# Attention on one Trainium2 core: heads paired in two 64-row halves of the array, a shared ring of three two-bank PSUM units, and q and k loaded per batch

## What is computed

```python
q = q.reshape(B, T, nh, hd)            # layer 0: rotated by cos, sin; layer 1: x @ Wq.T + bq
scores = jnp.einsum('bqhd,bkhd->bhqk', q, k) * scale + bias[None]   # the bias in layer 0 alone
attn = jax.nn.softmax(scores, axis=-1)
out = jnp.einsum('bhqk,bkhd->bqhd', attn, v)
```

## Time and profile before

| | us |
|---|---|
| median of 3 runs (lowest, highest) | 1241.4 (1240.12, 1244.76) |
| span of the profiled execution | 1240.9 |
| attention 0: until the first maxima, until the first scores, end | 53.6, 79.6, about 306 |
| attention 1: start, first maxima, first scores, last steps | 566, 621.5, 659.2, 912 |

### The profile page before, as it was taken

One profiled execution on the slowest core, in us unless ns is written; L12 is line 12 of the kernel. 1 busy time (PEld: TensorE's weight loads), 2 busy tenths in 40 slices (PEclk: granted clock), 3 DMA queues, 4 the chain that ended last, 5 costly groups with the idle time before them and its releaser, 6 DMA issues. The chain is left out here.

```text
span 1240.9 us, 15672 instructions
## 1 busy us (share of the span) xinstructions
PE 968.8 (78%) x5344; PEld 675.0 (54%) x5344; DVE 710.9 (57%) x1399; ACT 463.2 (37%) x702; POOL 350.5 (28%) x308
## 2 busy tenths in 40 slices
PE   0299999997609999973389999999976049999990
PEld 0144444453608999971245545656436038888880
DVE  6578888783610111108457777787614957667762
ACT  1026666666202323321015566565732104233320
POOL 7333333001051111113010101100010056888861
PEclk9999999999558999996568999999995559999995
DMA  9876655620338999954491555443005024454525
GB/s 191 150 141 124 115 80 108 83 31 10 109 140 293 342 336 353 337 210 148 95 145 30 102 82 106 70 58 54 7 1 204 0 81 119 111 148 128 122 37 152
DMA packets 83893, 159.87 MB, mean 129 GB/s; under 512 B 10088, under 2 KB 51944, under 8 KB 75624
## 3 DMA queue, kind: packets, MB, share of 16 engines
q1 hardware_dynamic: 74176, 142.13, 44.6%
q0 software_dynamic: 8384, 14.96, 5.7%
q10 hardware_dynamic: 1280, 2.10, 1.3%
HBM read 121.25 MB, written 35.80 MB: 127 GB/s over the span
## 5 line engine op out<-in xcount | busy, mean ns | idle before, releaser
L700 DVE TENSOR_REDUCE a_row_max<-ps_max 128x1 f32<-128x512 f32 x512 | 334.8, 686 | 95.5 <-PE ps_max L480 92.5
L594 ACT ACTIVATE a_probs<-ps_st 128x1024 f32<-128x1024 f32 x256 | 250.7, 1022 | 130.9 <-PE ps_st L496 129.2
L480 PE MATMUL ps_max<-a_ka,a_qa 96*128 96x512 f32 x512 | 221.2, 475 | 39.3 <-DMA a_ka<-scratch_k_scr 26.2
L480 PEld LDWEIGHTS ps_max<-a_ka,a_qa 96*128 96x128 f32 x512 | 96.8, 202 | 171.0 <-DVE a_row_max L700 124.2
L496 PE MATMUL ps_st<-a_qa,a_ka 104*128 104x512 f32 x512 | 173.7, 425 | 1.0 <-ACT a_probs L594 1.0
L510 PE MATMUL ps_out<-a_probs,a_vaug 128*32 128x512 f32 x1024 | 136.9, 607 | 0.4 <-ACT a_probs L594 0.4
L496 PEld LDWEIGHTS ps_st<-a_qa,a_ka 104*128 104x128 f32 x512 | 91.1, 193 | 23.4 <-ACT a_probs L594 8.7
L905 ACT ACTIVATE e_hid<-ps_st,e_wts 128x128 f32<-128x128 f32 x192 | 54.8, 369 | 114.6 <-PE ps_st L958 77.3
L1282 PE MATMUL ps_st<-e_xt,e_wr 128*128 128x512 f32 x384 | 93.6, 401 | 4.1 <-DVE e_xt L1344 2.7
L958 PEld LDWEIGHTS ps_st<-e_xst,e_wts 128*128 128x128 f32 x768 | 92.0, 196 | 2.2 <-issue 1.0
L958 PE MATMUL ps_st<-e_xst,e_wts 128*128 128x128 f32 x768 | 92.2, 280 | 0.6 <-DVE e_xst L1041 0.6
(11 more groups left out here) (184 smaller groups left out, 1149.4 us busy)
## 6 DMA issues: line engine op xcount, KB each, us to landing
e_wts<-in_w SPq DMA_DIRECT2D x24, 1156.0 KB, 8.1
e_wts<-in_w SPq DMA_DIRECT2D x24, 1024.0 KB
e_wf<-in_w SPq DMA_DIRECT2D x16, 1024.0 KB, 4.9
a_qa<-scratch_q_scr SPq DMA_DIRECT2D x96, 128.0 KB, 5.1
a_ka<-scratch_k_scr SPq DMA_DIRECT2D x96, 128.0 KB, 5.6
scratch_k_scr<-a_kst SPq DMA_DIRECT2D x16, 512.0 KB, 6.9
scratch_q_scr<-a_qst SPq DMA_DIRECT2D x64, 128.0 KB, 1.9
a_ctx_t<-in_ctx_t SPq DMA_DIRECT2D x8, 512.0 KB, 6.1
```

The lines of the kernel that those rows point to most:

```text
L480: pe.matmul(m.ps_max[:, n % 2], qa[0:MAX_ROW, g, h, qt * P:(qt + 1) * P], ka[0:MAX_ROW, g, h], start=True, stop=True).then_inc(mx_full, 1)
L594: nc.scalar.activation(probs[:, t % 3, 2 * pair:2 * pair + 2], m.ps_st[:, 2 * (n % 2):2 * (n % 2) + 2], ACT.Exp).then_inc(exp_done, 1)
L700: dve.tensor_reduce(row_max[:, s % 3, h, qt:qt + 1], m.ps_max[:, n % 2], AX.X, ALU.max).then_inc(mx_read, 1)
```

## The change

- A matmul now contracts 48 rows (52 with the bias), or 52 and 56 with the maxima rows. Even heads lie in partitions 0 to 63, odd heads in 64 to 127; the two matmuls of a pair follow each other, each in its own 64-row half, into the two banks of one unit.
- Six PSUM banks form a ring of three two-bank units, which maxima and scores take in turn. A unit is written once its user of three places before has been read. A DVE reduction reads both banks at once.
- Within a step the order is: maxima pair, scores pair, maxima pair, the first scores pair of the next step, `weigh`, then all jobs.
- q is handled in pairs of tiles (512 columns in `ps_misc`): ACT writes the high part, DVE the rest; POOL's subtraction is gone. In layer 0 the second pair of batch 0 is rotated by DVE. The scale moves from q into the exponential.
- `ka` and `qa` have two copies over batches and aren't cleared. Batch 0 is loaded by groups (12 DMAs of 64 KB each), every later batch at once (12 DMAs of 256 KB), and its first maxima wait for all twelve. SP, no longer ACT, issues the maxima rows, as two DMAs.
- The constant rows go in by six DMAs (two in layer 1) of 4 partitions and 128 KB from POOL at the start.
- The loads of x for batches 2 and 3 and the context of batch 1 are issued after the first loads of q and k; the statistics of batches 1 to 3 are computed in steps -5 and 4 (layer 0). The reciprocal root, in all four stages, has three rounds instead of four.

```diff
+def ring_schedule(steps):
+    ...
+    for t in steps:
+        if t == 0:
+            add("s", 0)
+        for half in range(2):
+            if 0 <= t + AHEAD < STEPS:
+                add("m", 2 * (t + AHEAD) + half)
+            if 0 <= 2 * t + half + 1 < 2 * STEPS and t >= 0:
+                add("s", 2 * t + half + 1)
...
+                def load(b, g, n):
+                    if g == 0:
+                        sp.wait_ge(k_stored, 32 * (b + 1))
+                        for j in range(2):
+                            sp.wait_ge(q_stored[j], 32 * (b + 1))
+                        if b >= 2:
+                            sp.wait_ge(st_full, 8 * NG * (b - 1))
+                    heads = slice(g * HG * HD, (g + n) * HG * HD)
+                    for par in range(2):
+                        for r, (qpart, kpart) in enumerate(((0, 0), (1, 0), (0, 1))):
+                            rows = slice(par * HALF_P + HD * r, par * HALF_P + HD * (r + 1))
+                            for dst, src in ((qa, q_scr[b, qpart, heads]), (ka, k_scr[b, kpart, heads])):
+                                sp.dma_start(dst[rows, b % 2, g:g + n].rearrange("d g p t -> d (g p) t").bitcast(F32),
+                                             src.rearrange("(h e d) t -> e d h t", e=2, d=HD)[par]).then_inc(loaded[g], 16)
...
-                            if t == 16 * b - 12 + 4 * g:
-                                load_group(b, g)
+                        if job[0] == "m":
+                            load_max(job[1])
+                    for b in range(1, B):
+                        if t == (4 if b == 1 else 16 * b - 13):
+                            load(b, 0, NG)
...
+                        pool.dma_start(dst[rows].rearrange("r f g p t -> r f (g p t)"),
+                                       src.unsqueeze(1).to_broadcast([4, 2, NG * PAIR * T])).then_inc(rows_in, 16)
...
+                def take_unit(kind, n):
+                    at = place[kind, n]
+                    if at >= 3:
+                        was, k = owner[at - 3]
+                        if was == "m":
+                            pe.wait_ge(mx_read, k + 1)
+                        else:
+                            pe.wait_ge(exp_done, k + 1)
+                    return unit(kind, n)
...
-                    scores(t, 0)
-                    maxima_scores(t + 8, 0)
-                    scores(t, 1)
-                    maxima_scores(t + 8, 1)
+                    maxima_scores(2 * (t + AHEAD))
+                    if t >= 0:
+                        scores(2 * t + 1)
+                    maxima_scores(2 * (t + AHEAD) + 1)
+                    if t >= 0:
+                        scores(2 * t + 2)
                     if 0 <= t - 1 < STEPS:
                         weigh(t - 1)
-                    for job in jobs[t][:-1]:
-                        run[job[0]](job)
-                    maxima_scores(t + 8, 2)
-                    maxima_scores(t + 8, 3)
-                    for job in jobs[t][-1:]:
+                    for job in jobs[t]:
                         run[job[0]](job)
...
+                    dve.wait_ge(mx_full, n + 1)
+                    dve.tensor_reduce(row_max[:, s % 3, qt, :, p], unit("m", n), AX.X, ALU.max).then_inc(mx_read, 1)
```

More of the change, by code:

```diff
@@ L367, in _ @@
                     keys(0)
-                    for i in range(TB):
-                        split_q(i)
                 for t in LT[1:]:
@@ L480, in maxima_scores @@
-                    pe.matmul(m.ps_max[:, n % 2], qa[0:MAX_ROW, g, h, qt * P:(qt + 1) * P], ka[0:MAX_ROW, g, h],
-                              start=True, stop=True).then_inc(mx_full, 1)
-                def scores(t, pair):
-                    if not 0 <= t < STEPS:
+                    if w == 0:
+                        pe.wait_ge(loaded[g], load_value(b, g))
+                    to = take_unit("m", n)
+                    for par in range(2):
+                        rows = slice(par * HALF_P, par * HALF_P + M_ROWS)
+                        ins = pe.matmul(to[:, par], qa[rows, b % 2, g, p, qt * P:(qt + 1) * P], ka[rows, b % 2, g, p], start=True, stop=True)
@@ L494, in scores @@
[L494 to L497 removed]
+                    if kc == 0 and p == 0:
+                        pe.wait_ge(max_in[s % 2], 32 * (s // 2 + 1))
+                    to = take_unit("s", n)
+                    for par in range(2):
+                        rows = slice(par * HALF_P, par * HALF_P + S_ROWS)
+                        ins = pe.matmul(to[:, par], ka[rows, b % 2, g, p, kc * P:(kc + 1) * P], qa[rows, b % 2, g, p], start=True, stop=True)
@@ L583, in _ @@
                     act_job(job)
-                    if job[0] == norm_kind and job[1] + 2 < TB:
-                        normed(job[1] + 2)
-                act.wait_ge(rows_in, 16 * n_rows)
                 for t in LT[1:]:
                     if 0 <= t < STEPS:
-                        for pair in range(2):
-                            n = 2 * t + pair
+                        for half in range(2):
+                            n = 2 * t + half
                             act.wait_ge(st_full, n + 1)
@@ L728, in _ @@
                     dve_job(job)
-                tile_stats(1, B)
+                if layer == 1:
+                    tile_stats(1, B)
                 for t in LT[1:]:
-                    for qt in range(TB):
-                        maxima(t + 8, qt)
-                        for job in (jobs[t][:-1] if qt == 1 else jobs[t][-1:] if qt == 3 else []):
-                            dve_job(job)
+                    for half in range(2):
+                        maxima(2 * (t + AHEAD) + half)
+                    if layer == 0 and t == -5:
+                        tile_stats(1, 2)
+                    if layer == 0 and t == 4:
+                        tile_stats(2, B)
+                    for job in jobs[t]:
+                        dve_job(job)
 def moe_top1(nc, m, dram):
```

368 lines of the change are left out of this document (192 added, 176 removed).

## The result

The changed kernel takes 1379.3 us (median of 4 runs, 1375.8 to 1387.6) against 1242.8 for the kernel before: 1.1115 times as long, 95% interval 1.1086 to 1.1143. It is slower, as forecast, by 38 us more than the 1341 of the sum. The profiled execution spans 1375.2 us.

A forecast was written before the change was run, and what follows sets the result against it. PE's own stream was taken to pace the steps, transfers and short chains the starts. Against the profile's 1240.9 us: 8 + 24 + 30 + 20 + 6 + 5 - 6 - 2 + 15 = +100, so 1341; own range 1286 to 1385.

The forecast's parts named there:

- steps, layer 0: Attention of layer 0: steps of 3.52 us, 0.14 over 3.38, for the 56 steps with maxima: +8 us.
- steps and jobs, layer 1: Attention of layer 1: steps of 4.4 us with jobs and their answers, 0.45 over 3.95, 56 steps: +24 us.
- loads: Batch loads at 119 GB/s stall PE: 18.5, 6 and 6 us in layer 0 (30), 16.5, 2 and 2 in layer 1 (20).
- first scores of layer 0: Start of layer 0: first maxima rows queue on SP behind loads, context and x; 86 against 79.6 us: +6.
- statistics in step 4: Layer 0, step 4: statistics of 8 tiles hold DVE some 6 us: +5 after its slack.
- layer 1's start: Before layer 1's attention: half as many reductions and a q round of two tiles shorten the start: -6 us.
- The loop over a reduction and `weigh`: Each step: maxima, reduction, scores pair and `weigh` run one behind the other, 3.17 us against 3.21, so nothing is won.
- the serial halves: Rival on maxima and scores pairs: the array halves don't overlap, each pair costs 0.26 us more; 1380 us, chance 0.12.
- The faster rival: DVE, not the loop, sets steps: about 1175 us, chance 0.14; needs a loop under 2.9 us and loads above 250 GB/s.
- clock term: PE at half clock after each of six stalls, 2.5 steps each: 18 us, of which +15 taken.
- slow-clock rival: The clock stays at half through the steps of both attentions: +110 us, 1450 us, chance 0.17.
- The bound of the prediction: Layer 1's jobs: nothing where DVE's slack takes all answers, twice as much where two jobs of a step queue.

The follow-up runs named there:

- run 6: The changed kernel with the first scores pair of each step computed three times over into the same unit: 1349.9 us.
- run 3: The changed kernel with `weigh` issued ahead of the next step's first scores pair: 1341.8 us.
- run 1: The changed kernel with q and k loads of batches 1 to 3 issued by groups of four heads, first maxima waiting for their own group: 1327.0 us.
- run 4: The changed kernel with both matmuls of each pair in one half of the array, odd heads' scores left out: 1514.1 us.
- run 9: The changed kernel with grouped loads, early `weigh`, early first maxima rows, threefold first scores pair to step 53, batch 1's context first, batch 2's jobs apart: 1254.1 us.
- 7: The changed kernel with only the even head's matmul of each step's first scores pair computed three times, in one array half: 1365.2 us.
- run 5: The kernel before, with maxima and scores matmuls contracting 52 rows in place of 96 and 104, exponential's input scaled by 0.01: 1448.4 us.

## Why the prediction was right, and where it was too low

| term | forecast | measured |
|---|---|---|
| steps, layer 0 | +8 | 0.16 a step in job-free slots, +9; the six q pairs +3 to 4 more |
| steps and jobs, layer 1 | +24 | about +38, with some half clock in it |
| loads | +30, +20 | waits of 30.9 and 16.0 |
| first scores of layer 0 | +6 | +7.4, and 4.5 more to the first `weigh` |
| statistics in step 4 | +5 | step of 8.48 in place of 3.9 |
| layer 1's start | -6 | -16.5 |
| last steps (54 on) | none | -4.2, -3.5 |
| root | -2 | not told apart (stretch behind attention 1: +2.5) |
| clock | +15 | at least 29 (run 6); about 40 as the rest of both layers |

**Right by its own steps.** The loop over a reduction and `weigh` sets the step: seen in the rows, and shown by run 3, which broke it and won 38. The batch load at some 110 GB/s: landed in 29.1 us for 28.5, and the rows behind it late by 8.8 and 7.7 for 6; run 1 took these away. That the waits add up to the forecast is in part luck: batch 1's was 14.4 for 18.5 in layer 0, and layer 1 had 8.5, none and 7.5 for 16.5, 2 and 2. The first scores at 87.0 for 86: the maxima rows are cast at 68.7, issued at 77.88 behind the loads, and there 9 us later. The total of 1379.3 is also the very 1380 of the serial halves, so the time alone would not have told the two apart; run 4 refutes that rival. The faster rival failed on both of its conditions, the loop of 3.34 us and loads at 108 GB/s.

**The step that failed in size is the clock term.** I put half clock behind six stalls, 2.5 steps each. Run 1 took all stalls away and 157 of 205 us at half stayed, and in run 6 the stalls stayed and more than half of the cold time went. So it is not the stalls alone that bring the clock down but also the steps that jobs and statistics lengthen, in which PE pauses for 1 to 2.8 us. My text set the slow-clock rival against this at 0.17 with the argument that PE at half would be "denser"; the window at 222 us shows that it is denser (4.23 of 4.70) and is still at half. The truth lay between forecast and rival: the clock held in job-free stretches, once reached, and was slow to come back. The size by difference: of the 65.5 us that attention 0 lost, the terms above and the first `weigh` explain 48, of the 75.4 of attention 1 53; the rest is about 40 us, an estimate.

**Layer 1's jobs were second**: 38 for 24. That figure is run 6's: its steps 0 to 53 took 281.8 us against 223.2, and 20.8 of the difference are DMA waits. Attention 1 of that run is still at half clock in 44 us, part of them in those waits, so 38 is a little too much for the jobs alone. The bound of the prediction names the cause: "twice as much, where two jobs of a step queue". The step with a v and a q job in the changed kernel, PE and DVE (fp32 matmuls, full clock):

```profile
797.69 1.99 PE L475 MATMUL ps_misc<-a_wv,a_ctx_t 128*128 128x256 f32 x8
...
799.72 0.69 DVE L720 TENSOR_TENSOR a_vaug<-ps_misc,a_bv 128x512 f32<-128x512 f32 x1 [2.05 <-PE ps_misc L475]
800.52 1.99 PE L458 MATMUL ps_misc<-a_xnt,a_wq 128*128 128x256 f32 x8 [0.84 <-DVEq L724]
...
804.42 0.50 PE L520 MATMUL ps_ring<-a_ka,a_qa 48*128 48x512 f32 x2 [1.24 <-ACT a_probs L639]
```

Two times 1.99 of PE, 0.84 of waiting for the one bank `ps_misc`, and ACT's answer ahead of an exponential: 9.49 us, where the kernel before, with a maxima pair between the jobs, had no step over 5.5. Splitting these jobs (run 9) turned 5.64, 4.71 and 8.60 us into 3.37, 4.72 and 4.71, and two steps of 3.05 into 4.12 and 5.75: 2.4 us won.

**Errors the other way** hid part of this: layer 1's start won 10 more than I gave it, and the last steps, where no maxima run, 7.7 that I had left out. The +8 for layer 0 is in part luck too: it set 3.52 against 3.38, a mean in which the short last steps count; steps 0 to 53 took 193.9 us before, 3.59 each, and 3.47 without other jobs than m and o, against 3.63 now. The wait of step 0 for POOL I had not looked at: I followed the late context on SP's queue, not to the engine that uses it.

Open stays what decides the clock's level. Runs 1, 6 and 7 show that PE's pauses, and what fills them, move it; runs 4 and 5 point to the rows in use (in 5 the values changed as well). The two layers of run 5, and the job-free steps of the changed kernel, show both levels with much the same work.

## What to carry to other kernels

When an edit makes an engine's work shorter, follow the buffers' ring, not the busy time: with four uses a step and three units, a step is a unit's fill and reading plus the longest stretch of the engine's own order, and moving an instruction only changes which reader is in it. Loads that are merged save issues, but everything behind them on the queue waits for the whole; split them or put small urgent rows ahead, and ask which engine waits for what was put behind. And matmuls that get narrower or rarer may cost TensorE's clock: read PEclk by stage before and after, and try whether redundant matmuls in its waits make the kernel faster.

## What the hardware showed that I had not expected

- Fewer rows with the same instructions: 96 and 104 cut to 52 (and with them the values read) took attention 0 from 223 to 389 us, at half clock with TensorE busy without a break.
- 512 redundant matmuls made a kernel 29 us faster (1379.3 to 1349.9).
- The issue of two small DMAs on ScalarE's queue took 1.33 us and held its next exponential; on SP the same two took 1.35 and kept no exponential waiting.
- A DVE instruction of 128x16 took 2.28 us beside POOL's rotation of the keys, 0.17 without it.
